# Storing the split weights of a gated-recurrent layer in DRAM during the first tile of time steps and reading them back in the other three

## The reference, cut to what matters

```python
xn = _layernorm(x)                                   # x: (8, 2048, 1024)
proj = xn @ w_in.T ; gate, xa = split(proj)          # w_in: (2048, 1024)
xc = causal_conv4(xa) + b_conv
forget, inp = split(xc @ w_gates.T + b_gates)        # w_gates: (2048, 1024)
alpha = exp(-8 * softplus(forget_base) * sigmoid(forget))
beta  = sqrt(1 - alpha**2 + 1e-6)
h = linear_scan(alpha, beta * sigmoid(inp) * xc)     # over time
s = (gelu(gate) * h) @ w_out.T                       # w_out: (1024, 1024)
logits = xn @ sel_w.T      # 8 selectors for each of 1024 outputs
comp   = xn @ comp_w       # 8 candidates for each of 1024 outputs
out = x + s * silu(comp[argmax(logits)])             # for each output
```

## Time and profile before

| | |
|---|---|
| median of 2 runs | 3816.59 us (3808.18 to 3824.99) |
| the profiled execution | 3810.57 us |
| its span on the slowest core (core 7) | 3808.7 us |
| spans of the eight cores | 3792.5 to 3808.7 us |
| granted TensorE clock, mean | 0.977 to 0.978 of 2.4 GHz |
| TensorE busy | 3584.6 us, 94% |
| POOL, DVE, ACT busy | 1556.1, 1618.2, 1152.0 us |

### The profile page before, as it was taken

How to read it: one execution, slowest core, us unless ns; L and a number is a source line. 1 busy time by engine, 2 the same in 40 slices (tenths; PEclk the granted TensorE clock), 3 DMA queues, 4 the chain that set the end, 5 groups by cost and what they waited for, 6 DMA issues and landing times.

```text
span 3808.7 us, 46753 instructions; the slowest of 8 cores (3792.5 to 3808.7 us)
## 1 busy us (share of the span) xinstructions
PE 3584.6 (94%) x16272; PEld 1596.6 (42%) x16272; DVE 1618.2 (42%) x1696; ACT 1152.0 (30%) x1323; POOL 1556.1 (41%) x784
## 2 busy tenths in 40 slices
PE   2999999999889999999978999999997999999997
PEld 0444444444334444443433444444343444444443
DVE  1536333333644433342464533344256353444333
ACT  1362322222136222222214522222221552222221
POOL 2345444443245444444324544444332444444442
PEclk8999999999989999999989999999998999999998
DMA  2234333332233333332233333333223333333332
GB/s 78 78 100 133 100 100 100 103 108 76 91 111 100 122 100 104 106 100 89 89 100 100 119 107 107 100 100 100 78 89 111 110 101 100 100 100 104 107 100 78
DMA packets 366872, 380.62 MB, mean 100 GB/s; under 512 B 12304, under 2 KB 356384, under 8 KB 366640
## 3 DMA queue, kind: packets, MB, share of 16 engines
q1 hardware_dynamic: 364032, 369.15, 30.8%
q0 software_dynamic: 2608, 8.49, 0.7%
HBM read 369.20 MB, written 8.39 MB: 99 GB/s over the span
## 4 chain that ended last, share of the span: by engine, by line
PE 84%; DVE 9%; DMA 3%; issue 1%; POOL 1%; ACT 1%; SPq 0%; DVEq 0%; ACTq 0%; POOLq 0%
PE pg L273 82%; DVE poolC L86 3%; DMA poolA<-xT 3%; DVE poolB L86 1%; DVE xnl L86 1%; DVE mxb L86 1%; POOL wl L86 1%; PE pg L343 1%; PE pg L337 1%; DVE msk L86 1%; DVE accb L86 1%; DVE xnh L86 1%; DVE xcl L86 0%; ACT xa L86 0%; DMA hb<-xT 0%
## 5 line engine op out<-in xcount | busy, mean ns | idle before, releaser
L86 POOL TENSOR_TENSOR wl<-w,wh 128x1024 bf16<-128x1024 f32 x672 | 1476.9, 2198 | 2076.7 <-ACT wh L86 2024.8
L273 PE MATMUL pg<-xnh,wh 128*128 128x512 bf16 x4608 | 1756.6, 381 | 124.3 <-DVE xnl L86 65.2
L273 PE MATMUL pg<-xnl,wh 128*128 128x512 bf16 x4608 | 1756.6, 381 | 0.0
L273 PE MATMUL pg<-xnh,wl 128*128 128x512 bf16 x4608 | 1756.1, 381 | 0.0
L86 ACT ACTIVATE wh<-w 128x1024 bf16<-128x1024 f32 x672 | 710.2, 1057 | 1621.3 <-PE pg L273 1550.6
L86 DVE TENSOR_SCALAR si<-pg,vecsb 128x512 f32<-128x512 f32 x256 | 192.1, 750 | 1415.1 <-PE pg L273 1414.7
L273 PEld LDWEIGHTS pg<-xnh,wh 128*128 128x128 bf16 x4608 | 452.9, 98 | 683.7 <-issue 147.2
L273 PEld LDWEIGHTS pg<-xnh,wl 128*128 128x128 bf16 x4608 | 452.9, 98 | 550.2 <-issue 11.8
L273 PEld LDWEIGHTS pg<-xnl,wh 128*128 128x128 bf16 x4608 | 452.7, 98 | 547.4 <-issue 10.7
L86 DVE SCALAR_TENSOR_TENSOR msk<-sf,vecsb,mxb 128x512 uint8<-128x512 f32 x256 | 292.6, 1143 | 27.4 <-DVE msk L86 0.9
L273 PE MATMUL pg<-xch,wh 128*128 128x512 bf16 x768 | 291.1, 379 | 0.7 <-POOL wl L86 0.7
(11 more groups left out here) (56 smaller groups left out, 920.1 us busy)
## 6 DMA issues: line engine op xcount, KB each, us to landing
w<-selT SPq DMA_DIRECT2D x256, 512.0 KB, 4.8
w<-cmpT SPq DMA_DIRECT2D x256, 512.0 KB, 4.8
w<-w1T SPq DMA_DIRECT2D x64, 512.0 KB, 4.7
w<-w2T SPq DMA_DIRECT2D x64, 512.0 KB, 4.7
w<-w3T SPq DMA_DIRECT2D x32, 512.0 KB, 4.8
hb<-xT POOLq DMA_DIRECT2D x32, 256.0 KB, 5.8
poolA<-xT SPq DMA_DIRECT2D x32, 256.0 KB, 3.5
outT<-poolC SPq DMA_DIRECT2D x32, 256.0 KB, 2.3
```

The source lines that it names most:

```text
L86: return fn(*a, **k)
L273: last = tensor.matmul(bank[:, :], wop[:, wcol:wcol + P], xop[:, k * TT:(k + 1) * TT], start=(idx == 0), stop=(idx == 23))
```

## The change

In tile 0 each half is fetched and split as before; then POOL issues two stores that write `wh` and `wl` (512 KB each) to a new DRAM tensor `wscr` of 84 × 128 rows of 4096 bf16. From tile 1 on there is neither fetch nor split: `pump_dma` returns at once, and `pump_split` issues two loads on SP's queue, straight from `wscr` into `wh[par]` and `wl[par]`, 4 KB for each partition. SP waits there for the last matmul group that used the pair (`whl_free`) and for the stores of that residue (`gw0` to `gw2`); `mm_group` waits for the loads (`wds0` to `wds2`). In tile 0 ACT also waits for the stores of the half three back before it overwrites `wh`. `w32` is not used after tile 0.

```diff
+    wscr = nc.dram_tensor("wscr", [84 * P, 2 * 8 * 256], BF16).ap()
@@ pump_dma
                 q = hs % 2
+                HF = 4 * HW
+                if hs >= NH:
+                    return
@@ pump_split
+                if hs >= NH:
+                    hrow = hs % NH
+                    wdn = "wds" + str(par)
+                    c.needt(sync, "sync", whl_free[par])
+                    c.need(sync, "sync", "gw" + str(hrow % 3),
+                           c.cnt["gw" + str(hrow % 3)])
+                    for pc, buf in ((0, wh), (1, wl)):
+                        ins = sync.dma_start(
+                            out=buf[par][:, :],
+                            in_=wscr[hrow * P:(hrow + 1) * P,
+                                     pc * 2048:(pc + 1) * 2048])
+                        c.inc(ins, wdn, 16)
+                    w_ready[par] = [(wdn, c.cnt[wdn])]
+                    return
                 lo_toks = []
                 for pc in range(2):
...
                     c.needt(scalar, "sc", whl_free[par])
+                    c.need(scalar, "sc", "gw" + str(par), c.cnt["gw" + str(par)])
                     ins = scalar.activation(
...
                 w_ready[par] = lo_toks
+                gwn = "gw" + str(par)
+                for pc, buf in ((0, wh), (1, wl)):
+                    ins = gpsimd.dma_start(
+                        out=wscr[hs * P:(hs + 1) * P, pc * 2048:(pc + 1) * 2048],
+                        in_=buf[par][:, :])
+                    c.inc(ins, gwn, 16)
```

More of the change, by code:

```diff
@@ L43, in __init__ @@
         for name in ("wd0a", "wd0b", "wd1a", "wd1b",
+                     "gw0", "gw1", "gw2", "wds0", "wds1", "wds2",
                      "gx", "gr", "go", "gv",
@@ L186, in build @@
         prev_silu_tile = [None]
+        scr_dma_tok = {}
         @block.vector
@@ L208, in pump_dma @@
                     c.needt(sync, "sync", tok)
-                HF = 4 * HW
                 for pc in range(2):
@@ L740, in _ @@
             gpsimd.wait_ge(c.h["gv"], c.cnt["gv"])
-            for s4 in ("wd0a", "wd0b", "wd1a", "wd1b"):
+            for sg in ("gw0", "gw1", "gw2"):
+                gpsimd.wait_ge(c.h[sg], c.cnt[sg])
+            for s4 in ("wd0a", "wd0b", "wd1a", "wd1b", "wds0", "wds1", "wds2"):
                 sync.wait_ge(c.h[s4], c.cnt[s4])
```

## The result

The changed kernel takes less time, by less than was forecast: the ratio of its times to those of before is 0.984, with a 95% interval of 0.981 to 0.987. That is clear of noise, but it stays under the 2% at which the prediction counted a change as faster. Its profiled execution took 3746.57 us (span 3744.7 us on core 7) against 3810.57 us (span 3808.7 us). What is left lies at 3744 to 3763 us, and at 3808 to 3825 us for the kernel before. The forecast was 3734 us.

What follows compares the result with a forecast made beforehand. TensorE bounds the kernel, busy 3584.6 of 3808.7 us, so gains lie in its gaps and the clock lost behind them. Span 3808.7 − 67 (crossings) − 19 (LNs) + 8 (start) + 1.2 (LN(1)) = 3732, time 3734 us; range 3708 to 3768.

Steps and rivals of the forecast that it cites:

- start: Kernel start: stores of the first halves and their issues delay the first x, +8 us, bounds 2 and 15.
- LN(1) squares: LN(1), after tile 0: the squares wait in POOL's queue behind two more store issues, +1.2 us.
- LN(2), LN(3): Later LNs: POOL is idle and the first two squares are ready, 2 × 9.5 = 19 us gained.
- first crossing: Tile boundary, end of w3T to start of w2T: 102.4 instead of 124.8 us, as at all three crossings.
- end: Last tile: last load behind combine 0's store, landed about when TensorE needs it; 0 us, bounds −3 and +4.
- seven more: 34.5: At each crossing: the seven combine steps after the first store, each store, load and add in a row, take 34.5 us.
- Moved: the loads behind the combines: Crossings: weight loads queue on SP behind eight combines, so TensorE runs out of weights; crossing gains 22.4 us, bounds 15.5 to 26.7.
- DVE beside POOL: Crossings: without POOL's subtractions DVE gains 12.6 us, so the 13.5 us gap for xnl shrinks to about 1.
- Stores in tile 0: Tile 0: 168 stores from POOL, 0.54 us per issue, bounds 0.54 and 1.1, hidden by TensorE within the tile.
- rival C: Tile 0: slow store issues, from 3.9 us, make POOL the bound; 3897 us, 2.3% slower; chance 0.05.
- Rival A: Crossings and start: loads land in series, start 15 us later; 3762 us, within 2%; chance 0.25.
- Rival B: Crossings: the load needed fourth lands sooner or undisturbed DVE shortens the combines; 3712 us, far better; chance 0.1.

Runs made afterwards that it cites:

- the run with the dummies: The changed kernel plus two unused POOL subtractions 128x1024 for each half of tiles 1 to 3; spans 3812.5 to 3826.0 us on cores 4 to 7.

## Why the prediction was right or wrong

The direction, the places and the mechanism were right, and 3746.6 us lies in the range of 3708 to 3768 us. But I held "faster by over 2%" the likeliest (0.55), and it came to 1.6%, which was the case with 0.4. Two things did that. The first is the size of one term, the chain of combines, with the landing of the loads behind it, below. The second is how I weighed the forecast: I had seen that it lies on the 2% line and yet counted it three to one as beyond it. A median of two runs, 3816.6 us, spoke for that, but one of the two stands alone at 3825; the ten of the later executions of the kernel before that are kept lie at 3807.7 to 3811.7. Against 3809 us the forecast was 2.0%, and the two sides of the line should have had about equal chances.

Term by term, on core 7:

| term | forecast | measured |
|---|---|---|
| start | +8 | +6.9 (x landed 55.3 against 48.4) |
| LN(1) squares | +1.2 | +1.5 (gap 7.8 against 6.3) |
| LN(2), LN(3) | −19 | −16.9 (13.8 us each, no gap; before 22.1 and 22.4) |
| first crossing | 102.4 | 111.5 |
| second crossing | 102.4 | 102.2 |
| third crossing | 102.4 | 106.8 |
| end | 0 | +0.3 (start of the last matmul to last instruction 25.7 against 25.4) |
| span | 3732 | 3744.7 |

*The failed step* is the size of the crossing's gain, 22.4 us times three, and in it above all "seven more: 34.5". The three crossings last 320.5 us together, where the forecast has 307.2. Here are its four pieces, on core 7, counted from the end of the last `w3T` matmul, so that each crossing is 0.4 us shorter than above:

| piece of a crossing | forecast | first, second, third |
|---|---|---|
| end of `w3T` to the first store | 8.4 | 9.2, 7.5, 9.1 |
| first to last store ("seven more") | 34.5 | 40.8, 34.0, 36.0 |
| last store to TensorE's restart | 5.8 | 7.2, 7.1, 6.8 |
| from there to `w2T` | 53.7 | 53.9, 53.2, 54.5 |

So the chain of combines accounts for 7.3 of the 13.3 us (6.3 more at the first crossing, 0.5 less at the second, 1.5 more at the third), and the landing of the two loads (0.46 + 4.8 us in the prediction) for 3.7. Against the kernel before, the crossings gave back 54.8 us and not 67. The LNs gave 16.9 and not 19, because I took the 23.3 us of LN(1) for the other two as well, and the start cost 1 to 2 us less than forecast. Together this is the way from 3732 to 3744.7. I took the 34.5 from one crossing and one core. The other cores of the same trace had 32.2 to 37.7 us in it, so the term deserved a range of its own, and it had none: in my range only what stands around the chain could vary. The chain is made of the landing of small transfers, whose times depend on what else moves: a load of x and a store took 3.6 and 2.3 us in the changed kernel and 4.9 and 2.8 us beside the weight loads. Why it was longest at the first crossing is open in part, as said above.

*Moved: the loads behind the combines.* Right in kind: issued 0.4 us behind the last store, gap of 16.5 to 19.5 us (forecast 17). The x of the first combine, behind 1 MB of weights, let the first store be issued at 7.5 to 9.2 us behind the end of `w3T` (forecast 8.4). The two loads took 6.6 us to land at the second crossing, with two more pairs issued right behind them, where I had 5.3; this is within my bounds, but late at all three.

*DVE beside POOL.* Right: the gap for `xnl` was 6.4, 0.8 and 1.2 us (forecast 7, 1, 1), and the run with the dummies brings it back. I had written that this was not what decides; the same run says it would, if POOL worked during the combines as well.

*Stores in tile 0.* Right, and rival C wrong: the issue from POOL took 554 and 547 ns at the median, 765 at most, where C needed 3.9 us.

```profile
L87 POOL DMA_DIRECT2D wscr<-wh x84: 554/554/593, 21.2 to 993.6; - x84
L87 POOL DMA_DIRECT2D wscr<-wl x84: 547/547/765, 21.8 to 994.2; - x84
```

The Trainium skill's page "SBUF — State Buffer", section "SBUF: two separate sides", says that DVE's fast copies can shut GpSimd out of writing descriptors. No run here tests it: none of a core's 168 issues met a DVE cast, on any of the eight. Most met DVE instructions with two operands, and beside those the longest issue took 0.77 us. So the narrow spread of x's issues, which the prediction held against this rule, did not speak to it either. Between its first weight matmul and LN(1), TensorE had no gap on any core, though a fetch of 512 KB took 8.8 us to land there instead of 4.8: two halves of lead are 20 us.

```profile
w<-selT SPq DMA_DIRECT2D x64, 512.0 KB, 8.8
```

*Rival A* (within 2%, by loads in series and a late start) had the right class, but its two terms did not come: the start came 7 us later and not 15, and the pair of loads landed 1.3 us later and not 4.8. *Rival B* hoped for a shorter chain of combines once DVE is undisturbed; it named the right place, and was rightly refused, as the chain is transfers. It took an edit of the chain itself.

## What to carry to other kernels

Taking work off helpers that are not the bound pays only where the bound engine waits, so cost it there: here three crossings and two LNs, 64 us for 1900 us of saved work on three helpers. A prefetch that is moved to a shared queue gets its deadline from what stands in front of it; look there for waits on other engines, and if that chain is made of transfers, take it apart first (each slot its own semaphore, load ahead, store not awaited): 57 us without any other change, and 72 on top of this one. And a term that is a chain of small transfers needs a range from several cores and crossings, not one reading.

## What the runs showed of the hardware

Transfers of one core slow each other's landing long before its DMA engines are full (their mean share at the crossings of the changed kernel was 0.37 to 0.39): with the weight loads beside them, core 7's eight combines took 48.7, 46.2 and 42.4 us instead of 40.8, 34.0 and 36.0. POOL subtractions whose result nobody waits for made the whole kernel about 2% slower, by way of DVE's two-operand instructions (0.69 us alone, 2.4 to 2.7 us beside one) and of the LN's squares behind them in POOL's queue. And one core of each pair had combines of 39 to 41 us at the first crossing where the other had 34 to 36. It was not the neighbour's stores; 3 of these 5 us fall in the step during which the neighbour issued six weight loads, and the rest is open.
